# Linear attention in the first phase of a decoder kernel: unsplit queries as the stationary operand, tokens on the partitions, and the result turned

## What is computed

```python
q = split_heads(x @ Wq.T); k = split_heads(x @ Wk.T); v = split_heads(x @ Wv.T)   # 16 heads of 32
q = elu(q) + 1.0
k = elu(k) + 1.0
kv_state = einsum('bhnd,bhne->bhde', k, v)        # 32 x 32 for each head
k_state = k.sum(axis=2)
attn_out = einsum('bhnd,bhde->bhne', q, kv_state)
denom = maximum(einsum('bhnd,bhd->bhn', q, k_state), 1e-06)[..., None]
local = xp[:, :-2] * conv_w[:, 0] + xp[:, 1:-1] * conv_w[:, 1] + xp[:, 2:] * conv_w[:, 2] + conv_b
out = (attn_out / denom + local) @ Wp.T + bp      # and x is added to it
```

## Time and profile before

| | |
|---|---|
| median of three runs | 3221.08 us (3220.52 to 3221.13) |
| the profiled execution | 3220.54 us, its span 3218.8 us |
| busy, share of the span | PE 98%, DVE 57%, ACT 42%, POOL 32% |
| chain that ended last | PE 94%, DVE 2%, ACT 1%, POOL 1%, issue 1% |
| granted TensorE clock, mean | 0.996 |
| the first phase | from the start to about 920 us |

### The profile page before, as it was taken

The page is one execution under the profiler, slowest core; times in us unless marked ns, Lnnn a source line. Parts: engine busy times, 40 slices in busy tenths (PEclk is TensorE's granted clock), DMA queues, the critical chain, the costliest instruction groups (busy, mean ns, idle before and its releaser), DMA issues.

```text
span 3218.8 us, 41066 instructions
## 1 busy us (share of the span) xinstructions
PE 3165.3 (98%) x15748; PEld 2655.7 (83%) x15748; DVE 1822.6 (57%) x3797; ACT 1350.2 (42%) x2575; POOL 1017.4 (32%) x838
## 2 busy tenths in 40 slices
PE   7999999999989999999999989999999999999998
PEld 6888888888877888888888878888888888888887
DVE  5666675757578787787788775232322323222564
ACT  4444434444446666666666652111211112111232
POOL 1332324232346666666666650000000000000243
PEclk9999999999999999999999999999999999999999
DMA  3112121212131211211211231000000000100343
GB/s 108 40 40 79 40 79 40 79 40 67 66 126 41 93 68 54 93 68 54 93 68 54 79 105 53 14 14 14 17 23 14 14 14 16 53 0 14 127 161 131
DMA packets 102867, 189.29 MB, mean 59 GB/s; under 512 B 6929, under 2 KB 13073, under 8 KB 102673
## 3 DMA queue, kind: packets, MB, share of 16 engines
q1 hardware_dynamic: 102672, 186.68, 16.4%
HBM read 136.33 MB, written 50.33 MB: 58 GB/s over the span
## 4 chain that ended last, share of the span: by engine, by line
PE 94%; DVE 2%; ACT 1%; POOL 1%; issue 1%; DMA 0%; POOLq 0%; ACTq 0%; DVEq 0%
PE c_p L132 11%; PE c_p L130 11%; PE c_p L131 11%; PE a_p L130 6%; PE a_p L131 6%; PE a_p L132 6%; PE b_n L130 4%; PE b_n L132 4%; PE b_n L131 4%; PE b_t L1593 3%; PE a_r L132 2%; PE a_r L130 2%; PE a_r L131 2%; PE b_l L132 2%; PE b_l L130 2%; PE b_l L131 2%
## 5 line engine op out<-in xcount | busy, mean ns | idle before, releaser
L1213 POOL TENSOR_SCALAR b_soft<-b_soft,b_one_in_sum 128x512 f32<-128x512 f32 x256 | 401.1, 1568 | 304.9 <-DVE b_one_in_sum L1396 304.9
L1796 ACT ACTIVATE c_gate<-c_p,c_bias 128x512 f32<-128x512 f32 x180 | 124.2, 690 | 732.0 <-PE c_p L132 732.0
L1830 DVE TENSOR_TENSOR c_gate<-c_gate,c_gate 128x512 f32<-128x512 f32 x64 | 44.3, 692 | 536.4 <-ACT c_gate L1796 536.4
L344 POOL TENSOR_TENSOR kept_scale<-c_ln_ve,minus_half 128x4 f32<-128x4 f32 x16 | 16.1, 1009 | 897.1 <-DVE c_ln_ve L336 897.1
L1415 DVE TENSOR_TENSOR b_p_lo<-b_t,b_p_hi 128x512 fp32r<-128x512 f32 x256 | 175.2, 684 | 166.6 <-ACT b_p_hi L1270 164.1
L1261 ACT ACTIVATE b_soft<-b_soft,b_minus_top 128x512 f32<-128x512 f32 x256 | 185.3, 724 | 190.4 <-DVE b_minus_top L1407 185.7
L570 ACT ACTIVATE a_elu<-a_p 128x512 f32<-128x512 f32 x128 | 76.6, 598 | 331.6 <-PE a_p L132 283.3
L1270 ACT ACTIVATE b_p_hi<-b_t 128x512 fp32r<-128x512 f32 x256 | 151.4, 591 | 107.7 <-PE b_t L1593 107.7
L2014 POOL TENSOR_TENSOR d_x<-d_x,d_y 128x512 f32<-128x512 f32 x64 | 82.8, 1295 | 295.0 <-ACT d_y L2026 295.0
L1407 DVE CUSTOM_DVE_ANT_0 b_soft<-b_l,b_mask_row 128x512 f32<-128x512 f32 x256 | 175.2, 684 | 0.0
L1593 PE MATMUL b_t<-ident,b_soft 128*128 128x128 f32 x1024 | 156.4, 275 | 12.8 <-DVE b_p_lo L1415 12.3
(11 more groups left out here) (311 smaller groups left out, 10035.9 us busy)
## 6 DMA issues: line engine op xcount, KB each, us to landing
a_x<-in_x SPq DMA_DIRECT2D x16, 1024.0 KB, 8.1
a_res<-in_x SPq DMA_DIRECT2D x16, 1024.0 KB, 6.1
x<-a_res SPq DMA_DIRECT2D x16, 1024.0 KB, 5.2
b_mem<-in_ctx SPq DMA_DIRECT2D x16, 1024.0 KB, 5.1
b_x<-x SPq DMA_DIRECT2D x16, 1024.0 KB, 5.7
b_res<-x SPq DMA_DIRECT2D x16, 1024.0 KB, 5.6
x<-b_res SPq DMA_DIRECT2D x16, 1024.0 KB, 4.6
c_x<-x SPq DMA_DIRECT2D x16, 1024.0 KB, 5.6
```

Of the source, the lines that this page charges most:

```text
L1213: pool.tensor_scalar(soft[:, at, :], soft[:, at, :], one_in_sum[:, at:at + 1], None, ALU.mult).then_inc(p_norm.sem, p_norm.unit)
L1796: act.activation(gate[j % 2][i][:, :], gating.banks[(3 * j + i) % 6][:, :], ACT.Tanh if g == "c" else ACT.Sigmoid, bias=added[:, i, j:j + ...
```

## The change

The attention of a block and a token tile becomes one full-precision product: the queries of 128 tokens (unsplit, 128 x 128) are the stationary operand, and the masked state of the block is the moving one, 128 columns of values and 4 of denominators, one for each head of the block (`KVW` 132). Tokens come out on the partitions with their own denominators beside them. There are 16 such blocks, three to a bank, in six groups (the last has one block). For each group VectorE makes a maximum, a reciprocal and a product with the reciprocal broadcast over each head's 32 channels (`attend(g)`). The result has channels along the row, so TensorE turns it back, four blocks for each of four channel blocks (`turn_att`), and VectorE adds the convolution to it.

The denominator products, the spreading products, the splits of queries, state and reciprocals go, with ScalarE's and GpSimd's passes for them. The five banks are handed out by `Rota` over 18 jobs in place of `Ring` over 20; the three banks have 14 jobs: six groups, four turned blocks, four output tiles.

```diff
-        KVW = P + HEADS
+        KVW = P + HC
+        BLOCKS, IN_BANK = C * T, 3
+        GROUPS = -(-BLOCKS // IN_BANK)
+        blocks_of = lambda g: range(IN_BANK * g, min(IN_BANK * (g + 1), BLOCKS))
...
-            q = [self.split(ctx, "a_q", [P, C, S])] * 2
+            q = sb("q", [P, C, S])
+            att = sb("att", [P, BLOCKS, P])
...
-            first = Ring(self.banks(held, "a_p", 5),
-                         [(rden_f, 0, 1)] + [(elu_out, t) for t in range(T)]
-                         + [(v_sb, t) for t in range(T)] + [(elu_out, T + c) for c in range(C)]
-                         + [(kv_part, 2), (kv_part, 5)] + [(tap2, c, -1) for c in range(C)] + [(kv_part, 5)], B)
-            K, V, Q, KV, TURN = 1, 1 + T, 1 + 2 * T, 1 + 2 * T + C, 3 + 2 * T + C
-            kq_bank = lambda u: first.bank(K + u if u < T else Q + u - T)
-            second = Ring(self.banks(held, "a_r", 3),
-                          [e for c in range(C) for e in ((spread_sb, c, 1), (att_sb, c, 1))]
-                          + [(x1_sb, t, 1) for t in range(T)], B)
-            SPREAD, OUT = 0, 2 * C
+            first = Rota(self.banks(held, "a_p", 5),
+                         [(elu_out, t, 0) for t in range(T)] + [(v_sb, t, 0) for t in range(T)] + [(elu_out, T + c, 0) for c in range(C)]
+                         + [(kv_sb, g, 0) for g in range(2)] + [(tap2, c, -1) for c in range(C)], B)
+            K, V, Q, KV, TURN = 0, T, 2 * T, 2 * T + C, 2 + 2 * T + C
+            kq_bank = lambda s, u: first.bank(s, K + u if u < T else Q + u - T)
+            second = Rota(self.banks(held, "a_r", 3),
+                          [(att_sb, g, 1) for g in range(GROUPS)] + [(z_f, c, 1) for c in range(C)] + [(x1_sb, t, 1) for t in range(T)], B)
+            ATT, TURNED, OUT = 0, GROUPS, GROUPS + C
...
-                        for c in range(C):
-                            pool.wait_ge(att_sb.sem, att_sb.upto(old.b, c))
-                            pool.tensor_tensor(att[c % 2][:, :], att[c % 2][:, :], local[old.par][:, c, :], ALU.add).then_inc(z_f.sem, z_f.unit)
...
-                    if new:
-                        for c in range(C):
-                            pool.wait_ge(q_hi.sem, q_hi.upto(new.b, c))
-                            pool.tensor_tensor(q[new.par].low[:, c, :], elu[:, c % 2, :],
-                                                       q[new.par][:, c, :].high_f32(), ALU.subtract).then_inc(q_lo.sem, q_lo.unit)
...
+                    def attend(g):
+                        n, blocks = len(blocks_of(g)), slice(blocks_of(g)[0], blocks_of(g)[-1] + 1)
+                        bank = second.bank(s, ATT + g)[:, 0:n * KVW].rearrange("p (i e) -> p i e", i=n)
+                        dve.wait_ge(att_ps.sem, att_ps.upto(old.b, g))
+                        dve.tensor_scalar(rden[:, blocks, :], bank[:, :, P:KVW], 1e-6, None, ALU.max).then_inc(rden_sb.sem, rden_sb.unit)
+                        dve.wait_ge(rden_sb.sem, rden_sb.upto(old.b, 2 * g))
+                        dve.reciprocal(rden[:, blocks, :], rden[:, blocks, :]).then_inc(rden_sb.sem, rden_sb.unit)
+                        if g == 0 and old.b >= 1:
+                            dve.wait_ge(attT_ps.sem, attT_ps.upto(old.b - 1))
+                        dve.wait_ge(rden_sb.sem, rden_sb.upto(old.b, 2 * g + 1))
+                        heads = lambda ap: ap.rearrange("p i (h e) -> p i h e", h=HC)
+                        dve.tensor_tensor(heads(att[:, blocks, :]), heads(bank[:, :, 0:P]),
+                                          rden[:, blocks, :].unsqueeze(3).broadcast_to([P, n, HC, HD]), ALU.mult).then_inc(att_sb.sem, att_sb.unit)
+                    s = new.b if new else old.b + 1
                     if old:
-                        dve.wait_ge(den_ps.sem, den_ps.upto(old.b))
-                        dve.tensor_scalar(rden[:, :], first.banks[0][0:HEADS, :], 1e-6, None, ALU.max).then_inc(rden_f.sem, rden_f.unit)
-                        dve.wait_ge(rden_f.sem, rden_f.upto(old.b, 0))
-                        dve.reciprocal(rden[:, :], rden[:, :]).then_inc(rden_f.sem, rden_f.unit)
+                        attend(0)
...
                         self.norm_tile(dve, N, after, x, 0)
                         self.norm_tile(dve, N, after, x, 1)
+                    if old:
+                        attend(1)
...
                     if after:
                         self.norm_tile(dve, N, after, x, 2)
                         self.norm_tile(dve, N, after, x, 3)
+                    if old:
+                        attend(2)
+                        attend(3)
                     if new:
                         elu_back(2)
                         weight_low(WQ, 0)
                     if after:
                         self.norm_variance(dve, N, after)
+                    if old:
+                        attend(4)
+                        attend(5)
+                    if new is None:
+                        for c in range(C):
+                            self.b_memory_low(dve, c)
                     if new:
                         elu_back(3)
...
                         for c in range(C):
-                            dve.wait_ge(spread_sb.sem, spread_sb.upto(old.b, c))
-                            dve.wait_ge(att_ps.sem, att_ps.upto(old.b, c))
-                            dve.tensor_tensor(att[c % 2][:, :], second.bank(SPREAD + 2 * c + 1)[:, :], att[c % 2][:, :], ALU.mult).then_inc(att_sb.sem, att_sb.unit)
+                            dve.wait_ge(attT_ps.sem, attT_ps.upto(old.b, c))
+                            dve.wait_ge(tap2.sem, tap2.upto(old.b, c))
+                            if c >= 2 or old.b >= 1:
+                                dve.wait_ge(z_lo.sem, z_lo.upto(*divmod(old.b * C + c - 2, C)))
+                            dve.tensor_tensor(z_sum[c % 2][:, :], second.bank(s, TURNED + c)[:, :], local[old.par][:, c, :], ALU.add).then_inc(z_f.sem, z_f.unit)
...
-                            bank = first.bank(KV + g)[:, 0:2 * (P + 2)].rearrange("p (c e) -> p c e", c=2)
-                            dve.tensor_tensor(kv_f[:, 2 * g:2 * g + 2, 0:P], bank[:, :, 0:P], kv_mask[:, :, :], ALU.mult).then_inc(kv_part.sem, kv_part.unit)
-                            for i in range(2):
-                                dve.tensor_scalar(kv_f[:, 2 * g + i, P:KVW], head_mask[:, 2 * g + i, :],
-                                                             bank[:, i, P:P + 1], None, ALU.mult).then_inc(kv_part.sem, kv_part.unit)
+                            bank = first.bank(new.b, KV + g)[:, 0:2 * KVW].rearrange("p (c e) -> p c e", c=2)
+                            dve.tensor_tensor(kv[:, 2 * g:2 * g + 2, :], bank, kv_mask[:, :, :], ALU.mult).then_inc(kv_sb.sem, kv_sb.unit)
...
-                    if old:
-
-                        if freed := first.freed(s, 0):
+                    def attend(t):
+                        for c in range(C):
+                            g, i = divmod(t * C + c, IN_BANK)
+                            if t == 0 and c == 0:
+                                if old.b == 0:
+                                    pe.wait_ge(raw.split_lo.sem, raw.split_lo.upto(WP))
+                                pe.wait_ge(elu_out.sem, elu_out.upto(old.b))
+                                pe.wait_ge(kv_sb.sem, kv_sb.upto(old.b))
+                            if i == 0 and (freed := second.freed(s, ATT + g)):
+                                pe.wait_ge(*freed)
+                            mm = pe.matmul(second.bank(s, ATT + g)[:, i * KVW:(i + 1) * KVW], q[:, c, t * P:(t + 1) * P], kv[:, c, :], start=True, stop=True)
+                            if t * C + c == blocks_of(g)[-1]:
+                                mm.then_inc(att_ps.sem, att_ps.unit)
+
+                    def turn_att(c):
+                        if freed := second.freed(s, TURNED + c):
                             pe.wait_ge(*freed)
-                        den_bank = first.bank(0)
-                        pe.wait_ge(kv_lo.sem, kv_lo.upto(old.b))
-                        for c in range(C):
-                            pe.wait_ge(q_lo.sem, q_lo.upto(old.b, c))
-                            mm = product(pe, den_bank[:, :], kv[old.par][:, c * KVW + P:c * KVW + 2 * P],
-                                         q[old.par][:, c, :], c == 0, c == C - 1)
-                        mm.then_inc(den_ps.sem, den_ps.unit)
+                        pe.wait_ge(att_sb.sem, att_sb.upto(old.b))
+                        for t in range(T):
+                            mm = pe.transpose(second.bank(s, TURNED + c)[:, t * P:(t + 1) * P], att[:, t * C + c, :], self.ident[:, :])
+                        mm.then_inc(attT_ps.sem, attT_ps.unit)
                     if new is None:
+                        for t in range(T):
+                            attend(t)
                         for c in range(C):
                             self.b_turn_memory(pe, c)
                     if new:
                         for t in range(T):
```

(63 more changed lines are left out.)

97 lines of the change are left out of this document (32 added, 65 removed).

## The result

The changed kernel took 3246.18 us (median of four runs, 3244.49 to 3250.7), the kernel before 3221.11 (3220.52 to 3221.68) beside it: a ratio of 1.008, 95% interval 1.0067 to 1.0093. It is slower by 25 us; 3246 was forecast. The profiled run took 3244.49 us.

What follows compares the result with a forecast made beforehand. TensorE's instruction stream was taken as the bound, without waits in a step. 3220.5 - 16.0 - 3.5 - 0.6 - 4.0 + 38.4 + 11.7 = 3246.5, stated as 3246 us; eight-in-ten range 3227 to 3262.

Steps and rivals of the forecast that it cites:

- Work on TensorE: TensorE's products per item: 6.51 us removed, full-precision products and turns added, net -1.07 us; -16.0 over 15 steps.
- The new wait: TensorE waits for groups 4 and 5, as VectorE's normalising stands behind load-bound statistics: 2.95 us in 13 steps, +38.4.
- The parts of the wait: Within each step, TensorE waits first 0.9 us for group 4, then 2.1 us for group 5.
- The clock: TensorE's granted clock falls after the idle stretches: nine of 13 steps lose 1.3 us, +11.7 (0 to 17).
- The start: Start of the phase: K tile 0 gets a free bank and waits only for its operands, -3.5 us (-2.5 to -4.2).
- The hand-over to step 1: Entering step 1: waits of 0.63 and 2.97 us go, K tile 0 waits for operands; -0.6 (+1 to -2).
- The last step: Last step of the phase: about +13.4 us where TensorE needed 18.25, partly at slow clock; -4 (-2 to -5).
- What costs nothing: VectorE has no more work in total; normalising beside GpSimd's additions, 1.140 instead of 0.541 each, adds 2.4 us under cover.
- Rival 1: VectorE has group 2 ready by block 15, so only the gain is left: 3196 us; chance 8%.
- Rival 2: Half a wait, near 1.8 us: short VectorE operations cost little and the load lands sooner; 3220 us, chance 6%.
- Rival 3: TensorE's added turns lower the clock: 1.3 us in each of 16 steps on top, 3267 us; chance 2%.

Runs made afterwards that it cites:

- both ends of the chain: Changed kernel with VectorE's groups 1 to 3 ahead of the next tokens' statistics, 3195.01 us; separately, with the tokens' load issued ahead of the store, 3197.45 us.
- two smaller doses: Changed kernel with TensorE's last K tile ahead of its last four attention blocks, 3207.2 us; separately, with only VectorE's second group ahead of the first two statistics, 3226.21 us.
- the groups first: Changed kernel with VectorE's attention groups 1, 2 and 3 moved ahead of the four statistics of the next item's tokens: 3195.01 us, ratio 0.992 to the kernel before.

## Why the prediction was right, step by step

- *Work on TensorE, -1.07 us a step.* Shown: 54.50 us a step without waits against 55.55, -1.05.
- *The new wait, 2.95 us in 13 steps.* Shown, and its cause with it, from both ends of the chain and by two smaller doses. The seven steps whose clock stayed high are 2.69 us over 54.50 on the mean. All 13 steps (756.26 us) are 47.8 over 13 x 54.50, 10.3 of it clock, so 37.5 of wait, against 38.4. The trace lists less idle time (31.4 us between 100 and 900), because it counts from the modelled end of a product. Read from start to start it is nearly all there (next point).
- *The parts of the wait.* The gap ahead of group 4 in the step shown is 545.74 less 544.10 and 0.227, 1.41 us, and that ahead of group 5 is 548.46 less 545.74 and six pieces of 0.113, 2.04. Over the 13 steps this gives 10.3 and 26.5, 36.8 of the 37.5. The second gap is 2.03 or 2.04 everywhere (forecast 2.1). The first (forecast 0.9) is 0.9 to 1.4 in nine steps and 0.1 to 0.2 in four, and the tokens decide which: they come 8.7 to 8.8 us after the step's start on TensorE in the four, 9.5 to 10.1 in the nine (10.05 in the step shown, 543.47 less 533.42, its first attention product), 9.43 on the mean, forecast 9.57. A group takes 0.92 us, 544.68 to 545.60 (0.98). The prediction's own terms give 14.56 less 11.53, 3.03 a step and not 2.95, a microsecond more over the 13 steps.
- *The clock, nine steps of 1.3 us.* It fell in six of 13, all among the nine with two waits. Each time 0.57 stood over four microseconds: 4 x 0.43 = 1.72 us of work lost. Six by 1.72 is 10.3, against 11.7: the number was too high and the price too low, and they cancelled.
- *The start, -3.5.* -3.7, of which 2.9 is shown to be the bank. The other 0.8 is no more than the first state products of two kernels with the old banks differ by (63.49 before, 62.72 before with the load moved). The reason had one flaw: I let K tile 0 wait for its last operand only and run at the lower clock before; its first products now start at 19.11, at full rate, and each three wait for their own operand.
- *The hand-over to step 1, -0.6.* Wrong by 2.0: with the work it came out at +0.4, not -1.7. The 0.63 and 2.97 of the earlier trace rows went, but K tile 0 waits three times (2.73 together) and the granted clock is 0.57 for eight microseconds, where the earlier trace rows has 0.55 for three. I had taken one moment for "operands ready" and had left the clock out.
- *The last step, -4.0.* -4.7; waits of 3.17 and 1.18 stand where 5.00 and 2.08 did.
- *What costs nothing.* Shown: with the groups first TensorE is busy for 54.50 of 54.50 us. The normalising (L350) takes 0.895 us on the mean in the kernel after, in place of 0.541, where 1.140 was forecast; the row behind that price is from phase B and does not say what ran beside it.
- *Luck.* The error at the hand-over (+2.0) and that of the fourteen steps (-2.1) cancel, and the four runs of the kernel after spread over 6 us, so that the median fell within 0.2 us of 3246 is chance. The mechanism and the size of its main terms are not.
- *Rival 1* had the size of the gain right (3196): it is what the kernel does once VectorE's order is mended, 3195.01. *Rival 2*'s half wait (3220) did not come: the whole wait did. *Rival 3* is refuted.

With the groups first the gains stand alone: 25.5 us by the spans (3218.8 less 3193.3), forecast 24.1. The losses are the rest: 49.5 (3242.8 less 3193.3), forecast 50.1.

## What to carry over

When a change gives a busy engine more to wait for, look at the order of the engine it will wait for: what stands ahead of the new releaser there, and what that waits for. A wait of an engine that isn't the bound costs nothing until something on the path is queued behind it; here a harmless wait for a load, 1.8 us a step on VectorE, came to stand ahead of 3 us on TensorE, and moving the groups ahead of it turned +25 us into -26. Price an idle stretch on TensorE with its clock, and expect the number of falls to vary.

## What the hardware showed

- The clock can fall after one idle stretch of 1.92 us in a stream that is otherwise full (0.57 from 312 to 316 us; another, of 1.98 us, gave 0.57 from 254 to 258), and stayed up after 2.38: three of 13 such steps fell in one run. With 0.75 to 1.27 us and then 1.77 us, and 0.94 us of busy time between, six of nine fell.
- A full-precision product with 128 x 132 as its moving operand is two pieces of 0.113 us, and lies between fp32r products without loss: step after step of 54.50 us.
- The reciprocal of 128 x 12 values took 0.23 us (a maximum of as many, 0.15), that of 128 x 4 took 0.18; the 16 x 512 one took 3.34. With the tokens on the partitions an item's reciprocals come to 5 x 0.23 and 0.18, 1.3 us.
